# Attention and mixture-of-experts layer on one core: projections from fp16 part sums, and expert tiles with gate and up computed features-on-partitions

## What is computed

```python
x = x + attn_ref(layernorm(x), qkv_w, qkv_b, out_w, out_b)
# ffn_ref(xf), xf = layernorm(x):
ffn(x, gw, uw, dw) = (silu(x @ gw.T) * (x @ uw.T)) @ dw.T      # 352 hidden features
shared = ffn(xf, shared_gate, shared_up, shared_down)
probs = softmax(xf @ gate_w.T); topw, topi = top_k(probs, 2); topw = topw / (topw.sum(-1) + 1e-20)
routed = sum over the 2 chosen of 8 experts: ffn(xf, gate[e], up[e], down[e]) * weight
x = x + shared + routed
```

## Time and profile before

| what | value |
|---|---|
| median of 3 runs | 928.4 us |
| the profiled execution, device time | 927.27 us |
| its span (first to last instruction) | 925.5 us |
| PE / DVE / ACT / POOL busy | 862.5 / 696.2 / 685.6 / 712.2 us |
| mean granted PE clock | 0.979 of full |

### The profile page before, as it was taken

The page is one execution under the profiler, slowest core; times in us unless marked ns, Lnnn a source line. Parts: engine busy times, 40 slices in busy tenths (PEclk is TensorE's granted clock), DMA queues, the critical chain, the costliest instruction groups (busy, mean ns, idle before and its releaser), DMA issues.

```text
span 925.5 us, 25699 instructions
## 1 busy us (share of the span) xinstructions
PE 862.5 (93%) x10266; PEld 595.1 (64%) x10266; DVE 696.2 (75%) x1771; ACT 685.6 (74%) x842; POOL 712.2 (77%) x448
## 2 busy tenths in 40 slices
PE   4788999999999999999999999999999798859996
PEld 3455667666666666666666676666666564438886
DVE  7798797888879797978797979796978356535445
ACT  4456788988898888888988898888889963114442
POOL 1466889998899889988988898888889967344442
PEclk9799999999999999999999999999999999879999
DMA  5121232323232424232301020202020001112214
GB/s 179 24 66 50 56 67 64 67 56 67 63 71 52 75 56 81 59 73 67 66 21 39 19 48 1 57 1 47 2 47 2 2 1 38 46 35 68 61 46 144
DMA packets 60149, 48.33 MB, mean 52 GB/s; under 512 B 8688, under 2 KB 57714, under 8 KB 59904
## 3 DMA queue, kind: packets, MB, share of 16 engines
q1 hardware_dynamic: 57760, 42.48, 20.3%
q0 software_dynamic: 2272, 4.22, 1.3%
HBM read 13.93 MB, written 16.29 MB: 33 GB/s over the span
## 4 chain that ended last, share of the span: by engine, by line
PE 61%; DVE 24%; issue 4%; POOL 4%; ACT 3%; DMA 2%; another core or an unknown queue 1%; SPq 0%; POOLq 0%; DVEq 0%; ACTq 0%
DVE row_max L1028 10%; PE st L1308 7%; PE st L1309 7%; PE bg L1233 6%; PE pv L1340 5%; PE pv L1342 4%; PE pv L1344 4%; POOL p_parts L585 4%; DVE junk L1024 3%; PE bg L1223 3%; PE bg L1483 3%; PE bg L1198 3%; PE bg L1199 2%; PE bg L1200 2%; DVE att_parts L1050 2%
## 5 line engine op out<-in xcount | busy, mean ns | idle before, releaser
L585 POOL TENSOR_TENSOR p_parts<-prob,p_parts 128x1024 f16<-128x1024 f32 x320 | 613.2, 1938 | 101.1 <-ACT p_parts L720 99.0
L719 ACT ACTIVATE prob<-st,p_bias 128x1024 f32<-128x1024 f32 x320 | 330.9, 1034 | 110.5 <-PE st L1309 78.6
L720 ACT ACTIVATE p_parts<-st,p_bias 128x1024 f16<-128x1024 f32 x320 | 330.3, 1032 | 0.0
L1028 DVE TENSOR_REDUCE row_max<-bg 128x1 f32<-128x512 f32 x384 | 250.5, 684 | 8.4 <-PE bg L1233 7.1
L1340 PE MATMUL pv<-v_parts,p_parts 128*128 128x65 f16 x2176 | 232.7, 193 | 3.1 <-POOL p_parts L585 2.6
L1342 PE MATMUL pv<-v_parts,p_parts 128*128 128x64 f16 x2176 | 233.0, 195 | 0.0
L1344 PE MATMUL pv<-v_parts,p_parts 128*128 128x65 f16 x2176 | 232.0, 192 | 0.0
L1308 PE MATMUL st<-qk_parts 128*128 128x512 f16 (+3 forms) x640 | 222.2, 350 | 5.8 <-ACT p_parts L720 3.5
L1340 PEld LDWEIGHTS pv<-v_parts,p_parts 128*128 128x128 f16 x2176 | 202.3, 96 | 28.0 <-DVE attn L1080 8.8
L1309 PE MATMUL st<-qk_parts 66*128 66x512 f16 (+3 forms) x640 | 220.3, 350 | 0.0
L1233 PE MATMUL bg<-qk_parts 128*128 128x512 f16 (+3 forms) x640 | 210.7, 352 | 9.5 <-DVE row_max L1028 2.2
(11 more groups left out here) (230 smaller groups left out, 1086.5 us busy)
## 6 DMA issues: line engine op xcount, KB each, us to landing
qk_parts<-qk_parts SPq DMA_DIRECT2D x192, 64.0 KB, 2.0
row_dram<-fill SPq DMA_DIRECT2D x8, 1290.0 KB, 10.3
qk_parts<-qk_parts SPq DMA_DIRECT2D x16, 256.0 KB, 3.0
stage_raw<-ffn_w SPq DMA_DIRECT2D x16, 176.0 KB, 2.6
v_parts<-row_dram SPq DMA_DIRECT2D x39, 64.5 KB
qk_parts<-y_dram SPq DMA_DIRECT2D x8, 256.0 KB, 4.7
w_raw<-qkv_w SPq DMA_DIRECT2D x8, 192.0 KB, 2.3
down_w<-ffn_w SPq DMA_DIRECT2D x1, 1536.0 KB, 8.2
```

The costliest lines, as they stand in the source:

```text
L585: nc.gpsimd.tensor_tensor(o, a, b, ALU.subtract).then_inc(p_lo_ready, 1)
L719: nc.scalar.activation(o32, src, ACT.Exp, bias=p_bias[:], scale=D ** -0.5)
L720: nc.scalar.activation(o16, src, ACT.Exp, bias=p_bias[:], scale=D ** -0.5).then_inc(exp_done, 1)
L1028: nc.vector.tensor_reduce(row_max[:, t, c:c + 1], bank, AX_X, ALU.max).then_inc(bg_drained, 1)
```

## The change

1. **Projections.** `xn_hi`, `xn_lo`, `att_parts` and `split` (the parts of the activations, the attention output and the weights) are fp16 in place of float32r. The instructions stay.
2. **Gate and up of the tiles.** The expert's columns are stationary and the tile's features move: for each of two halves (gate, up) and three chunks of 128 features, three products of 128 columns, 18 matmuls in place of 6. Each product's weights are sliced at their own place, by the register. The result has features on partitions, which is what `tile_down` needs; `turn_hidden`, its three transposes, `tile_hidden` and ACT's copy go. `tile_down` of tile i-1 stands where that of tile i-2 stood.
3. **Widths.** Gate and up are kept 384 wide (3 x 128, the last 32 columns zero) in place of 352: the loads, the staging by ACT and POOL, silu and the product.
4. **Waits.** ACT's silu waits for the gate half alone (`t_gate_ready`); DVE's product waits for silu, for the up half and for the down product of tile i-2.

```diff
-        att_parts = sb("att_parts", [P, 2 * BLK], F32R)
+        att_parts = sb("att_parts", [P, 2 * BLK], F16)
-        xn_hi = sb("xn_hi", [P, T], F32R)
-        xn_lo = sb("xn_lo", [P, T], F32R)
+        xn_hi = sb("xn_hi", [P, T], F16)
+        xn_lo = sb("xn_lo", [P, T], F16)
-        split = sb("split", [P, 12, P], F32R)
+        split = sb("split", [P, 12, P], F16)
...
-        stage_raw = sb("stage_raw", [P, F], F32)
-        experts = sb("experts", [P, EXPERTS, 4 * F], F16)
+        stage_raw = sb("stage_raw", [P, FW], F32)
+        experts = sb("experts", [P, EXPERTS, 4 * FW], F16)
...
-            for i in range(TILES + 2):
-                if i < TILES:
-                    act.wait_ge(t_gu_ready, i + 1)
-                    nc.scalar.activation(t_silu[i % 2], st[:, i % 2, 0, 0:F], ACT.Silu).then_inc(t_silu_done, 1)
-                if 1 <= i <= TILES:
-                    tile_hidden(i - 1)
+            for i in range(TILES):
+                act.wait_ge(t_gate_ready, i + 1)
+                nc.scalar.activation(t_silu[i % 2], st[:, i % 2, 0, 0:FW], ACT.Silu).then_inc(t_silu_done, 1)
                 if i + AHEAD < TILES:
                     tile_x_hi(i + AHEAD)
...
                     dve.wait_ge(t_silu_done, i + 1)
-                    nc.vector.tensor_tensor(t_h32[i % 2], t_silu[i % 2], st[:, i % 2, 1, 0:F], ALU.mult
+                    dve.wait_ge(t_gu_ready, i + 1)
+                    wait(dve, t_down_done, i - 1)
+                    nc.vector.tensor_tensor(t_h[i % 2], t_silu[i % 2], st[:, i % 2, 1, 0:FW], ALU.mult
                                             ).then_inc(t_h_done, 1)
...
-                nc.tensor.matmul(g, t_x_hi[i % 2], w_hi_e[:, 0:F], start=True, stop=False)
-                nc.tensor.matmul(g, t_x_hi[i % 2], w_lo_e[:, 0:F], start=False, stop=False)
-                nc.tensor.matmul(g, t_x_lo[i % 2], w_hi_e[:, 0:F], start=False, stop=True)
...
-            def turn_hidden(i):
...
+                for part, ready in enumerate((t_gate_ready, t_gu_ready)):
+                    for c in range(FC):
+                        out = st[:, i % 2, part, tile(c)]
+                        cols = slice(part * FW + c * P, part * FW + (c + 1) * P)
+                        high = gu_hi[:, bass.ds(e, 1), cols].rearrange("p o c -> p (o c)")
+                        low = gu_lo[:, bass.ds(e, 1), cols].rearrange("p o c -> p (o c)")
+                        nc.tensor.matmul(out, high, t_x_hi[i % 2], start=True, stop=False)
+                        nc.tensor.matmul(out, high, t_x_lo[i % 2], start=False, stop=False)
+                        mm = nc.tensor.matmul(out, low, t_x_hi[i % 2], start=False, stop=True)
+                    mm.then_inc(ready, 1)
...
                 for c in range(FC):
-                    k = min(P, F - c * P)
-                    mm = nc.tensor.matmul(t_y_bank, t_hidden[i % 2][0:k, tile(c)], weights[0:k, tile(c)],
+                    mm = nc.tensor.matmul(t_y_bank, t_h[i % 2][:, tile(c)], weights[:, tile(c)],
                                           start=(c == 0), stop=(c == FC - 1))
```

More of the change, by code:

```diff
@@ L11 @@
 from concourse import mybir
-F32, F32R = mybir.dt.float32, mybir.dt.float32r
+F32 = mybir.dt.float32
 F16, BF16, U32 = mybir.dt.float16, mybir.dt.bfloat16, mybir.dt.uint32
@@ L34 @@
 F, FC = 352, 3
+FW = FC * P
 EXPERTS = 8
@@ L295, in layer_kernel @@
         tail = pflat[:, (SRING + HRING) * BLK:]
-        t_silu = [tail[:, k * F:(k + 1) * F] for k in range(2)]
-        t_h32 = [tail[:, (2 + k) * F:(3 + k) * F] for k in range(2)]
+        t_silu = [tail[:, k * FW:(k + 1) * FW] for k in range(2)]
+        t_h = [tail[:, (2 + k) * FW:(3 + k) * FW] for k in range(2)]
         t_y = [p_words[:, EXPERTS * FC * P + k * P:EXPERTS * FC * P + (k + 1) * P] for k in range(YRING)]
-        t_hidden = [tail[:, 4 * F + k * FC * P:4 * F + (k + 1) * FC * P] for k in range(2)]
-        gu_hi, gu_lo = experts[:, :, 0:2 * F], experts[:, :, 2 * F:4 * F]
+        gu_hi, gu_lo = experts[:, :, 0:2 * FW], experts[:, :, 2 * FW:4 * FW]
         gathered = [v_words[1][:, k * ROW:(k + 1) * ROW] for k in range(XRING)]
@@ L696, in stage_high @@
                 act.wait_ge(stage_landed, 16 * (k + 1))
-                nc.scalar.copy(gu_hi[:, e, j * F:(j + 1) * F], stage_raw[:]).then_inc(stage_hi_ready, 1)
+                nc.scalar.copy(gu_hi[:, e, j * FW:(j + 1) * FW], stage_raw[:]).then_inc(stage_hi_ready, 1)
             def router_exps():
@@ L1163, in _ @@
             base_sum(3)
-            for i in range(TILES + 2):
+            for i in range(TILES + 1):
                 if i < TILES:
                     dve.wait_ge(t_silu_done, i + 1)
-                    nc.vector.tensor_tensor(t_h32[i % 2], t_silu[i % 2], st[:, i % 2, 1, 0:F], ALU.mult
+                    dve.wait_ge(t_gu_ready, i + 1)
+                    wait(dve, t_down_done, i - 1)
+                    nc.vector.tensor_tensor(t_h[i % 2], t_silu[i % 2], st[:, i % 2, 1, 0:FW], ALU.mult
                                             ).then_inc(t_h_done, 1)
@@ L1455, in gate_up @@
                     pe.wait_ge(h_ready, STEPS)
-                w_hi_e = gu_hi[:, bass.ds(e, 1), :].rearrange("p o c -> p (o c)")
-                w_lo_e = gu_lo[:, bass.ds(e, 1), :].rearrange("p o c -> p (o c)")
-                g, u = st[:, i % 2, 0, 0:F], st[:, i % 2, 1, 0:F]
-                nc.tensor.matmul(g, t_x_hi[i % 2], w_hi_e[:, 0:F], start=True, stop=False)
-                nc.tensor.matmul(g, t_x_hi[i % 2], w_lo_e[:, 0:F], start=False, stop=False)
-                nc.tensor.matmul(g, t_x_lo[i % 2], w_hi_e[:, 0:F], start=False, stop=True)
-                nc.tensor.matmul(u, t_x_hi[i % 2], w_hi_e[:, F:2 * F], start=True, stop=False)
-                nc.tensor.matmul(u, t_x_hi[i % 2], w_lo_e[:, F:2 * F], start=False, stop=False)
-                nc.tensor.matmul(u, t_x_lo[i % 2], w_hi_e[:, F:2 * F], start=False, stop=True).then_inc(t_gu_ready, 1)
-            def turn_hidden(i):
-                pe.wait_ge(t_h_done, i + 1)
-                wait(pe, t_hidden_ready, i - 1)
-                if i < 2:
-                    pe.wait_ge(bg_drained, BG_TOTAL)
-                for c in range(FC):
-                    k = min(P, F - c * P)
-                    mm = nc.tensor.transpose(bg[0:k, i % 2, tile(c)], t_h32[i % 2][:, c * P:c * P + k], ident[:])
-                mm.then_inc(t_turned, 1)
+                for part, ready in enumerate((t_gate_ready, t_gu_ready)):
[8 more added lines that the diff above has]
+                    mm.then_inc(ready, 1)
             def tile_down(i, e):
                 pe.wait_ge(down_landed, 16)
-                pe.wait_ge(t_hidden_ready, i + 1)
+                pe.wait_ge(t_h_done, i + 1)
                 wait(pe, t_y_ready, i)
@@ L1494, in _ @@
             pe.wait_ge(stage_lo_ready, len(STAGED))
-            for i in range(TILES + 2):
+            for i in range(TILES + 1):
                 if i < TILES:
                     gate_up(i, expert[i])
-                if 1 <= i <= TILES:
-                    turn_hidden(i - 1)
                 if i + AHEAD == EARLY:
@@ L1505, in _ @@
                     tile_x(i + AHEAD)
-                if i >= 2:
-                    tile_down(i - 2, expert.pop(i - 2))
+                if i:
+                    tile_down(i - 1, expert.pop(i - 1))
             pe.wait_ge(t_h_done, TILES)
-            pe.wait_ge(t_hidden_ready, TILES)
             pe.wait_ge(t_x_lo_ready, TILES)
```

17 lines of the change are left out of this document (6 added, 11 removed).

## The result

The changed kernel takes 949.4 us (median of four runs, 948.89 to 953.57), the kernel before 928.5 beside it. The ratio is 1.0235, with an interval of 1.0206 to 1.0264: 20.9 us slower. The forecast was 944.3, 15.9 slower, with a range of 921 to 956.

The account below looks back on a forecast made before the run. The prediction took PE to set the pace in attention, and PE's sequencer to become the tile loop's bound. Projections -8.9 and -0.3, staging +0.6 and the loop +24.5 gave +15.9: 944.3 us, read as 936 to 953, stated range 921 to 956.

Parts of the forecast that it names:

- The period: Expert loop, PE's sequencer: 2.0 us a tile plus 8 more address computations at 0.125, less one wait of 0.125: 2.875.
- A: Expert loop: PE's columns decide, as no more address computations are paid for than before; 1.88 a tile, 908.8 us; chance 0.10.
- B: Expert loop: each address computation costs only its recorded 46 ns; 2.24 a tile, about 922 us; chance 0.04.
- C: Expert loop: weight loads don't hide behind 128 columns, while the sequencer is cheap; 2.61 a tile, 935 us; chance 0.03.
- The row of the forecast: Earlier trace: four fp16 matmuls of 128 columns in 0.23 us, 0.057 each, taken as the price for gate and up.
- D: Expert loop: the second matmul on a slice computes its address again; 18 computations, 3.62 a tile, 972 us; chance 0.03.
- E: Expert loop: granted clock falls to 0.5 as PE idles; up to 3.76 a tile, 976 us; chance 0.05.
- Part 1: Projections in fp16: 0.14 us gained a task, -8.9 us in attention (-5 to -12) and -0.3 in the prologue.
- three quarters: Attention projections: share taken of the at most 12 us gain, part being lost where POOL or DVE is late; -8.9 us.
- Part 2: Staging 384 wide: POOL's instruction 855 to 933 ns, ACT's 504 to 550, 16 times; 0 to 1.9 us, taken as +0.6.
- Part 3: Tile on PE's columns: 18 matmuls 1.03 us for 0.90, transposes' 0.32 gone, down 0.74; 1.88 in place of 2.07.
- the stage ahead: The stall before the expert loop: taken to stay as it is; if it changed, worth -8 to +2 us.

Follow-up runs that it names:

- e3: Changed kernel with expert 0's gate and up weights in every tile, so no address computations for them: 918.7 us, ratio 0.9879, 2.04 us a tile.
- e4: Changed kernel with only the low parts fixed to expert 0, 6 address computations for gate and up instead of 12: 922.4 us, 2.25 us a tile.
- e12: Kernel before with fp16 projections and experts' weights staged 384 wide, old tile loop: 919.0 us, against 918.7 for the fp16 projections alone.
- e11: Changed kernel with six-operation address instructions spread between matmuls, loads of three numbers without range check, two PSUM buffers for down's result: 913.0 us, ratio 0.9831.
- e5: Kernel before with expert 0's gate and up weights in every tile, 4 address computations a tile less: 926.6 us, ratio 0.9984, 2.00 us a tile.
- e2: Changed kernel with the projections' parts back in float32r, so the tile loop's change alone: 958.8 us, ratio 1.0323 to the kernel before.
- e1_proj: Kernel before with only the four projection part types changed to fp16, old tile loop: 916.9 us, ratio 0.9872.
- e8_fused_before: Kernel before with fp16 projections and a tile's 7 addresses computed by 4 register instructions: 918.8 us, ratio 0.9908, 2.05 us a tile.
- e6: Changed kernel with a tile's 12 addresses computed in one place, in six register instructions of six operations: 928.1 us, ratio 0.9980, 2.35 us a tile.
- e9: Changed kernel with 12 addresses in six instructions and experts' numbers loaded for two tiles at a time without range check: 916.0 us, ratio 0.9865.
- e10: Kernel before with fp16 projections, fused addresses and experts' numbers loaded for three tiles at a time without range check: 918.1 us, ratio 0.9875.

## Why the forecast came out as it did

**The bound: right.** The sequencer, by 12 computations a tile. The rows it asked for are there: 12 of 46 ns, 0.13 apart, matmuls with a gap at each new slice, PE's idle put to issue, full clock, tiles 2.97 apart. e3 and e4 show the cause with a dose.

**The period: right in kind, 0.10 too low.** Forecast 2.875 (2.7 to 3.1), measured 2.97. 0.03 of it are the computations, 12 from 880.81 to 882.35 in 1.53 us and not 1.50. The remaining 0.07 lies in what was kept of the old sequence: its 2.0 was read off starts of one decimal in the earlier trace rows, where the period was 2.07. The 36 tiles from the third to the last: 76.9 us before, forecast 102.7, measured 105.6 by the starts of L1457 (825.3 to 930.9).

**Rivals: out.** A (columns, 1.88) is what remains when the computations are gone; it was no picture of this kernel. B (46 ns) would have been 2.24. For C, e3 runs the same weight loads at 0.056 us a matmul; the Trainium skill's 81 ns a matmul (TensorE: Matmul & The Clock Gate, section Back-to-back issue gap) is too long for this case, where every matmul has its weight load too. The row of the forecast was a mixed one (two of its four matmuls are in bf16 and one has 66 rows), and its 0.057 held all the same. D would show 18 computations. E: the loop kept its full clock with PE busy for 76.90 of 95.10 us.

**Part 1: mechanism right, 2 to 3.5 us too small.** -9.2 forecast with the prologue, -10.9 and -12.7 measured. The 0.14 us a task was right (0.82 to 0.68). The term that was mis-sized is "three quarters": 10.5 of 12 us came through in heads 1 to 15, as PE was the bound nearly everywhere.

**Part 2: +0.6 forecast, nothing that could be measured (0.3 in e12).** Both instructions grew, by less than costed (POOL 855 to 910 ns, where 933 was said, ACT 504 to 527, where 550 was said), and attention hid them.

**Part 3: the columns.** 1.88 forecast, 1.79 measured in e11; down takes 0.67 and not 0.74. The old shape's 2.07 was held to be columns; e5 shows 2.00 for them and 0.07 for the sequencer.

**The tiles' half as a whole: 5.5 us too small.** +25.1 forecast (24.5 and 0.6), +30.6 in e2. 2.9 are the period (105.6 against 102.7). At the loop's end 1.1 us were won and not 1.8, which is 0.7 (930.9 to 934.7 in place of 904.4 to 909.3). There the sum had no term for the last down product's wait, which is for DVE's copy of the tile before:

```profile
933.93 0.93 PE L1468 MATMUL bg<-down_w,prob 128*128 x6 [0.75 <-DVE p_parts L1152]
```

The rest, some 2 us, lies outside the loop, where the forecast had the stage ahead stay as it is, with -8 to +2 as its worth.

**The stage ahead of the loop** lies between the last exponential and the first silu. It lasted 58.3 us in the trace of before and 63.5 in that of the changed kernel (the rows of the result). The same stage of e2_tiles, then of e1_proj, then of e8_fused_before (the granted clock stands third from the right):

```profile
767.30:828.10 60.80, 47.97 (x218) 23.82 (x214) 30.07 (x125) 13.10 (x24) 34.57 (x34) 0.88 0.15 45
```

```profile
753.30:813.90 60.60, 47.09 (x195) 23.91 (x191) 29.93 (x125) 13.11 (x24) 34.45 (x34) 0.86 0.15 44
```

```profile
753.80:810.90 57.10, 45.58 (x198) 23.61 (x193) 30.21 (x126) 13.30 (x24) 31.94 (x32) 0.91 0.15 44
```

A clock of 0.90 over 58.3 us is 12 us at half (2 x 0.10 x 58.3), 0.84 over 63.5 is 20. Over all kernels the three shortest stages, 57 to 58 us, have 0.90 or 0.91, and the four longest, over 63 us, 0.84 or 0.85. Half clock is 1.2 GHz in place of 2.4. In the changed kernel one stretch at half clock is 13.7 us long where before had two of 3.4 us with a full one between them:

```profile
781.70:795.40 13.70, 12.28 (x26) 6.78 (x27) 6.66 (x42) 2.08 (x4) 0.91 (x1) 0.50 0.13 35
```

What starts and ends these stretches was not tested. The three kernels with float32r parts had 0.90, 0.91 and 0.88 in that stage, the eleven with fp16 parts 0.84 to 0.91, nine of them 0.87 or less. But that is one execution of each, and executions of one kernel differ as much: in 19 of the kernel before on one chip the mean granted clock of the whole run went from 0.970 (932.8 us) to 0.981 (925.6 us). By the medians of all executions the types don't differ: 0.974, 0.976 and 0.974 for the kernel before in its three groups, 0.973 and 0.977 for the fp16 projections alone. That the fp16 parts move the clock is not shown. The profiled execution of the changed kernel also ran its first head in part at half clock: 60.7 us from its first exponential to the next head's, 57.6 before and 56.8 to 59.2 in all others. With the longer stage ahead of the loop, 5.2 us, that is more than the 5 us that the two traces differ by over the medians. How long these stretches were in the executions without a trace is not known.

By the terms, in the trace of e2_tiles against that of before (spans 957.8 and 925.5, 32.3 us apart): 27.8 from the first silu to the matmuls behind the loop (113.4 against 85.6), 2.5 in the stage ahead (60.8 against 58.3), 2.1 in the heads (727.7 against 725.6, most of it in the first), and 0.1 less in what is left. The forecast had 24.5, nothing, 0.6 and nothing. The loop's term shows in the changed kernel's own trace too, with 26.9. The 2.5 and the 2.1 stand on one execution of each kernel and may be the clock's.

The total was 5.0 us too small. The tiles cost 5.5 us more than forecast, and the projections gave 1.7 to 3.5 more, which hid a part of it. By these two the miss would be 2 to 4 us; the rest of the 5.0 lies between medians of different groups and is not placed. That the total came as near as it did owes a part to two misses of opposite sign, which is luck; that the sequencer bounds the tiles is not.

## What to carry to other kernels

Count, per iteration, not only an engine's columns but also the instructions that its sequencer must work off itself, and read their price from start to start, not from the recorded duration. A slice at a run-time index costs an instruction for each distinct place: a change that makes operands smaller and more numerous multiplies them. If the shape is wanted all the same, compute the addresses together, so that few instructions carry them all: that alone gave 21 us here. Spreading these between matmuls was part of the fastest kernel, and its share is not shown.

## What the runs showed of the hardware that I had not expected

- A register instruction on PE's sequencer costs 0.12 us with three operations (12 in 1.53 us in the changed kernel) and 0.13 to 0.14 with six (e6); recorded are 46 and 74 ns. The number of instructions counts far more than that of operations.
- The load of one number into a register is recorded with 301 ns, of two with 551, of three with 769 (medians; e9 and e10). The check of its range with the assertion holds the sequencer for 0.28 us more (882.7 to 883.0 in the changed kernel), nearly the load again; without it, and with loads of two, a tile was 0.32 us shorter.
- In e5 a load of 0.30 us and its check were hidden in every tile (2.00, what the columns take). In e10 a load of 0.77 us was not: two tiles at 2.00, the third at 2.24.
- PE's loop kept its full granted clock (1.00) with PE busy for 76.90 of 95.10 us. Executions of one kernel, the one before, went from 924.8 to 932.8 us with a mean granted clock of 0.980 to 0.970.
- 128-column fp16 matmuls with a weight load each ran 0.056 us apart for a whole tile (18 in 1.00 us in e11, 850.38 to 851.38).
